# A graph network with 2376 indirect gathers: the gathers lose their bounds check

## The chip, the cores and the metric

The kernel runs on one core of a Trainium2 chip. The metric is device time in microseconds for one execution of the whole program, as the median of several runs.

## The reference

Four graph layers run one after the other on x [100000, 64] with the same 50000 edges (src, dst), sorted by dst. Each layer normalises x, applies relu, gathers rows by src or dst, combines them per edge, sums them per dst and adds the result to x.

```python
edge_index = jnp.stack([src, dst])
h = jnp.maximum(_layernorm(x, axis=-1), 0.0)
x = x + _L0_gnn_ref(h, node_type_4, src, dst, edge_type_8, ...)   # typed attention, softmax per dst
h = jnp.maximum(_layernorm(x, axis=-1), 0.0)
x = x + _L1_gnn_ref(h, proj_cosim, W_ffn, b_ffn, src, dst)        # h[src] - h[dst], gated, two segment sums
h = jnp.maximum(_layernorm(x, axis=-1), 0.0)
x = x + _L2_gnn_ref(h, edge_index, W0, b0, W1, b1)                # (h + segment_sum(h[src])) through an MLP
h = jnp.maximum(_layernorm(x, axis=-1), 0.0)
x = x + _L3_gnn_ref(h, Wq, ..., src, dst)                         # four attention heads
return x
```

## The kernel before

Nodes that no edge points to need no gathers, so their whole path is computed once for all nodes by a dense pass, and the rows of the nodes that do receive edges are then replaced by scatters at the end. The edges are padded to 50688, which is 99 groups of GE = 512, and a group is laid out as TU = 4 blocks of 128 edges, one edge per partition. The nodes are padded to 101376, 99 groups of 1024.

The program is a row of stages with a barrier between them: tables (L304), dense (L478), scores (L693), softmax, attend (L1019), difference (L1222), propagate (L1401), mlp (L1533) and heads (L1695). A stage writes its order out by hand: for every engine a `body` is called for each of the 99 groups plus a tail, and the groups are staggered between the engines by `st.back(lag)`. Everything is unrolled. The engines are kept in step by semaphores, with U = 3 buffers for a group's tiles.

All indirect DMAs are issued from POOL (the GpSimd engine), one for 128 rows, since an offset is given per partition:

- scores, L733: eight gathers a group from the table T0 (rows of 68 floats) into `sc_xg`, four by src and four by dst. POOL waits for `h_done` (DVE, L192), `ptr_c` and the write of the same buffer of three groups ago.
- difference, propagate, mlp, heads: four gathers a group through the helper `gather` (L1212, issue at L1217) from U1, SD, U2 and U3 (rows of 64 floats) into `df_hs`, `pr_gat`, `ml_gat` and `hd_gat`. POOL runs at most three groups ahead of the engine that uses up the rows.
- dense, L522: four scatters a group of two floats a row into T0; heads, L1743: four scatters a group of 64 floats a row into the output. An index far above the table's size marks an edge that writes nothing, and the bounds check drops it.

The indices of the gathers are computed in tables and softmax, and all of them lie inside their tables, padding included. For each indirect DMA with a bounds check the program holds an instruction ahead of it on POOL, a MOVE, that puts the bound into a register; where a group begins with a wait, the wait or the last of several stands on that MOVE.

## Time and profile before

| | us |
|---|---|
| three runs, median | 6802.56 |
| three runs, lowest and highest | 6772.72, 6810.67 |
| profiled execution, its own time | 6742.33 |
| profiled execution, span from the first to the last instruction | 6740.6 |

| Engine | busy us | share of the span |
|---|---|---|
| PE | 5010.8 | 74% |
| DVE | 4934.0 | 73% |
| POOL | 4537.2 | 67% |
| ACT | 2271.6 | 34% |

The profile is of one execution. An instruction's row tells when its engine worked on it; register, wait and branch instructions are not counted as busy. For a DMA that POOL issues, the busy time is POOL's and not that of the transfer. Idle time ahead of an instruction stands with the one that released it; "issue" means that nothing the profile shows was waited for. POOLq is POOL's sequencer. The mean granted clock of TensorE is 0.745 of full speed over the span.

### The profile page before, as it was taken

The page shows a single profiled execution, that of the slowest core. Times are in us where ns is not written, and L with a number is a line of the kernel's source. Part 1 is how long each engine was busy: PE and PEld are TensorE (multiplying, and loading weights), DVE is VectorE, ACT ScalarE, POOL GpSimd, SP SyncE. Part 2 cuts the span into 40 slices and gives each one's busy share as a digit, 9 for nine tenths or more (in the row PEclk, how much of TensorE's full clock was granted, in tenths as well). Part 3 has the DMA queues.
Part 4 walks back from the last instruction along what each step waited for, and adds up shares of the span by engine and source line. Part 5 has one row for each costly group of instructions (what it writes and reads, how often), then busy time and mean ns, then how long its engine had stood idle before and what let it go on. Part 6 is the DMA issues. An engine that isn't in the chain of part 4 may idle for free. (4 is left out here: it accounts for less than half of the span.)

```text
span 6740.6 us, 68483 instructions
## 1 busy us (share of the span) xinstructions
PE 5010.8 (74%) x17065; PEld 2596.9 (39%) x17065; DVE 4934.0 (73%) x7942; ACT 2271.6 (34%) x5856; POOL 4537.2 (67%) x3884
## 2 busy tenths in 40 slices
PE   0777777588888886888887887555577878878876
PEld 0455555344444442333334444122233334444433
DVE  4899999766766766999996665565566667666666
ACT  0555555322222222334333333122122223333333
POOL 1777777567767762666667887666566657777777
PEclk9777777789999997888885555555587767666676
DMA  9222222233333333555543332344455542222221
GB/s 352 85 95 94 95 94 95 80 71 77 77 77 77 79 72 82 145 143 144 142 132 84 82 82 74 95 106 107 96 140 140 141 122 62 65 65 66 63 58 42
DMA packets 788893, 673.28 MB, mean 100 GB/s; under 512 B 514176, under 2 KB 520906, under 8 KB 788376
## 3 DMA queue, kind: packets, MB, share of 16 engines
q1 hardware_dynamic: 486456, 459.62, 23.4%
q0 software_dynamic: 102464, 90.84, 8.1%
q10 hardware_dynamic: 199584, 118.45, 5.7%
q8 instruction: 145, 2.38, 0.1%
q14 instruction: 244, 2.00, 0.1%
HBM read 396.20 MB, written 276.35 MB: 100 GB/s over the span
## 5 line engine op out<-in xcount | busy, mean ns | idle before, releaser
L733 POOL DMA_INDIRECT sc_xg<-t,keep_gather x792 | 872.9, 1102 | 375.5 <-issue 246.0
L1217 POOL DMA_INDIRECT df_hs<-u,keep_idx x396 | 512.8, 1295 | 129.1 <-issue 108.8
L1217 POOL DMA_INDIRECT hd_gat<-u,keep_idx x396 | 481.7, 1216 | 155.4 <-issue 118.0
L1217 POOL DMA_INDIRECT ml_gat<-u,keep_idx x396 | 398.0, 1005 | 274.9 <-issue 125.5
L1743 POOL DMA_INDIRECT out_x<-hd_x,keep_scat_out x396 | 456.3, 1152 | 153.0 <-issue 119.5
L1217 POOL DMA_INDIRECT pr_gat<-sd,keep_idxsd x396 | 411.4, 1039 | 219.0 <-issue 128.9
L522 POOL DMA_INDIRECT t<-keep_ptr_pay,keep_scat_ptr x396 | 441.4, 1115 | 108.2 <-issue 105.2
L1193 PE MATMUL at_ps_m<-at_vx,keep_weights 128*64 128x512 f32 x792 | 446.8, 717 | 26.4 <-POOL at_vx L1090 26.4
L877 PE MATMUL sc_ps_r<-sc_qx,keep_weights 128*64 128x512 f32 x792 | 394.1, 644 | 84.8 <-DVE sc_prod L794 63.0
L687 PE MATMUL den_ps_m<-keep_weights,den_hid 128*128 128x64 f32 x1584 | 237.5, 313 | 199.6 <-ACT den_hid L643 199.6
L1205 PE MATMUL at_ps_y<-keep_weights,at_agg 64*128 64x256 f32 x792 | 239.0, 451 | 171.2 <-DVE at_ysel L1117 170.9
L1883 PE MATMUL hd_ps_h<-keep_weights,hd_xb 128*128 128x128 f32 x792 | 247.8, 413 | 130.9 <-DVE hd_wn L1826 126.0
L1090 POOL TENSOR_TENSOR at_vx<-at_eq,at_v 128x1024 f32<-128x1024 f32 x99 | 255.6, 2582 | 132.0 <-issue 79.5
L153 DVE SCALAR_TENSOR_TENSOR den_den_n_cent<-den_den_n_sum,den_x 128x512 f32<-128x512 f32 x198 | 334.1, 1687 | 3.6
L654 PE MATMUL den_ps_t<-keep_consts,den_h 128*128 128x128 f32 x792 | 185.1, 384 | 195.8 <-DVE den_h L192 195.5
L687 PEld LDWEIGHTS den_ps_m<-keep_weights,den_hid 128*128 128x128 f32 x1584 | 222.2, 224 | 241.4 <-ACT den_hid L643 241.3
L772 DVE SCALAR_TENSOR_TENSOR sc_qx<-sc_et,keep_consts,sc_ps_q 128x512 f32<-128x512 int32 x396 | 276.8, 740 | 48.1 <-DMA t<-tab_row 26.9
L1078 POOL TENSOR_TENSOR at_y<-at_ysel 128x512 f32<-128x512 f32 x99 | 137.4, 1388 | 245.8 <-DVE at_ysel L1117 245.8
L172 ACT ACTIVATE den_den_n_sq<-den_den_n_cent 128x64 f32<-128x64 f32 x792 | 190.6, 242 | 327.0 <-DVE den_den_n_cent L153 326.9
L1883 PEld LDWEIGHTS hd_ps_h<-keep_weights,hd_xb 128*128 128x128 f32 x792 | 195.7, 304 | 250.1 <-DVE hd_wn L1826 203.1
L871 PE MATMUL sc_ps_q<-sc_ht,keep_weights 128*128 128x512 f32 x396 | 223.3, 692 | 92.0 <-issue 68.3
L794 DVE TENSOR_TENSOR sc_prod<-sc_ps_r,sc_kv 64x512 f32<-64x512 f32 x99 | 67.6, 683 | 306.0 <-DMA tab_types<-in_node_type 202.2
(288 smaller groups left out, 13259.5 us busy)
## 6 DMA issues: line engine op xcount, KB each, us to landing
u<-den_h SPq DMA_DIRECT2D x198, 256.0 KB
t<-tab_row ACTq DMA_DIRECT2D x99, 272.0 KB, 11.3
tab_x<-in_x SPq DMA_DIRECT2D x99, 256.0 KB
den_x<-in_x SPq DMA_DIRECT2D x99, 256.0 KB
out_x<-den_x SPq DMA_DIRECT2D x99, 256.0 KB, 2.6
sc_et<-in_etype_row SPq DMA_DIRECT2D x99, 256.0 KB
at_v<-vt SPq DMA_DIRECT2D x198, 128.0 KB
at_et<-in_etype_row SPq DMA_DIRECT2D x99, 256.0 KB
```

Of the source, the lines that this page charges most:

```text
L153: v.scalar_tensor_tensor(out=self.cent[:, :, :], in0=self.over(self.sum), scalar=-1.0 / D, in1=x, op0=ALU.mult, op1=ALU.add).then_inc(self ...
L522: pool.indirect_dma_start(pairs, bass.IndirectOffsetOnAxis(ap=e.scat_ptr[:, c:c + 1], axis=0), e.ptr_pay[:, c, :], None, bounds_check=NP * ...
L687: m = pe.matmul(ps_m[:, j, :], hid[:, a, c * P:(c + 1) * P], e.W["w1"], start=(j == 0), stop=(j == RN - 1), skip_group_check=True)
L733: pool.indirect_dma_start(xg[i][:, u, :], None, e.T0, bass.IndirectOffsetOnAxis(ap=e.gather0[:, b.n, u:u + 1], axis=0), bounds_check=NP - ...
L772: return v.scalar_tensor_tensor(out=qx[:, r, :], in0=et[b.s][:, :], scalar=e.C["rels"][:, r:r + 1], in1=ps_q[:, :], op0=ALU.is_equal, op1= ...
L877: m = pe.matmul(ps_r[:, :], e.W["att"][:, r * D:(r + 1) * D], qx[:, r, :], start=(r == 0), stop=(r == 3))
L1090: pool.tensor_tensor(vx[i][:, 2:4, :], eq[i][:, :, :], vin[i][:, :].unsqueeze(1).broadcast_to([P, 2, GE]), ALU.mult).then_inc(vx_high, 1)
L1193: m = pe.matmul(ps_m[d.s][:, :], e.W["msg"][:, r * D:(r + 1) * D], vx[d.s][:, r, :], start=(r == 0), stop=(r == 3))
L1205: m = pe.matmul(ps_y[:, u, :, :], agg[f.s][:, u * P:(u + 1) * P], e.W["a"][0:D, :].rearrange("p (t f) -> p t f", t=4), start=(u % 2 == 0), ...
L1217: pool.indirect_dma_start(gat[i][:, u, :], None, table, bass.IndirectOffsetOnAxis(ap=idx_all[:, c:c + 1], axis=0), bounds_check=rows - 1, ...
L1743: pool.indirect_dma_start(e.out, bass.IndirectOffsetOnAxis(ap=e.scat_out[:, c:c + 1], axis=0), x4[i][:, u, :], None, bounds_check=NP - 1, ...
L1883: pe.matmul(ps_h[i][:, u, :], xb[i][:, u * P:(u + 1) * P], e.W["wfx"], start=(u == 0), stop=False, skip_group_check=True)
```

## The change

The 2376 gathers are issued without `bounds_check` and `oob_is_err=False`. The helper `gather` loses the argument `rows` that carried the bound. The two groups of scatters (L522 and L1743) are as they were. In the built program the MOVE ahead of each gather is gone, so POOL's MOVEs fall from 3168 to 792, and a wait that stood on a group's first MOVE stands on the gather itself; the gather's out-of-range mode goes from skipping to error. Otherwise every engine holds the same instructions in the same order, and no data, buffer or semaphore value differs.

```diff
@@ scores
                     for u in range(R):
                         pool.indirect_dma_start(xg[i][:, u, :], None, e.T0,
-                                                bass.IndirectOffsetOnAxis(ap=e.gather0[:, b.n, u:u + 1], axis=0),
-                                                bounds_check=NP - 1, oob_is_err=False).then_inc(gathered[i], 16)
+                                                bass.IndirectOffsetOnAxis(ap=e.gather0[:, b.n, u:u + 1], axis=0)).then_inc(gathered[i], 16)
@@
-def gather(pool, table, idx_all, gat, gathered, st, pos, rows):
+def gather(pool, table, idx_all, gat, gathered, st, pos):
 
     i = st.s
     for u in range(TU):
         c = pos * TU + u
         pool.indirect_dma_start(gat[i][:, u, :], None, table,
-                                bass.IndirectOffsetOnAxis(ap=idx_all[:, c:c + 1], axis=0),
-                                bounds_check=rows - 1, oob_is_err=False).then_inc(gathered[i], 16)
+                                bass.IndirectOffsetOnAxis(ap=idx_all[:, c:c + 1], axis=0)).then_inc(gathered[i], 16)
@@ difference (propagate, mlp and heads likewise)
-                    gather(pool, e.U1, e.idx1, hs, gathered, st, pos(st), 2 * EP)
+                    gather(pool, e.U1, e.idx1, hs, gathered, st, pos(st))
```

## Rows read from the trace of the kernel before

**Rows 1.** The page's first part: busy time, share of the span, instructions.

```profile
PE 5010.8 (74%) x17065; PEld 2596.9 (39%) x17065; DVE 4934.0 (73%) x7942; ACT 2271.6 (34%) x5856; POOL 4537.2 (67%) x3884
```

**Rows 2.** Busy time by stretch: scores, difference, heads.

```profile
core 0: us, PE busy (x) PEld busy (x) DVE busy (x) ACT busy (x) POOL busy (x), PEclk, DMA share, GB/s
...
1301.00:2545.00 1244.00, 1042.74 (x3863) 512.95 (x3864) 839.89 (x1367) 336.76 (x582) 872.94 (x792) 0.91 0.37 75
...
3551.00:4195.00 644.00, 526.35 (x1770) 304.60 (x1770) 419.98 (x496) 206.71 (x690) 512.76 (x396) 0.50 0.32 81
...
5522.00:6710.00 1188.00, 935.90 (x2740) 484.15 (x2740) 793.53 (x1268) 446.12 (x882) 922.02 (x776) 0.70 0.23 63
```

**Rows 3.** Groups of heads' POOL DMAs: count | busy, mean ns | idle before, releasers.

```profile
L1217 POOL DMA_INDIRECT hd_gat<-u,keep_idx x396 | 481.7, 1216 | 155.4 <-issue 118.0 <-POOLq L207 34.9 <-DVE hd_x L1821 2.4
L1743 POOL DMA_INDIRECT out_x<-hd_x,keep_scat_out x396 | 456.3, 1152 | 153.0 <-issue 119.5 <-DVE hd_x L1821 33.5
```

**Rows 4.** Waits in scores, propagate, mlp: total us, times, longest.

```profile
POOL sc_xg L733 <- DVE sc_h L192: 110.5, 28, 6.2
DVE sc_sc_n_sum L149 <- DMA sc_xg<-t,keep_gather: 23.7, 3, 15.9
...
POOL pr_gat L1217 <- DVE pr_gm L1481: 71.8, 16, 6.6
DVE pr_gm L1481 <- DMA pr_gat<-sd,keep_idxsd: 24.8, 5, 8.0
...
POOL ml_gat L1217 <- DMA xh<-at_xh: 60.9, 27, 3.7
POOL ml_gat L1217 <- PE ml_ps_t L1674: 60.3, 22, 3.2
PE ml_ps_t L1674 <- DMA ml_gat<-u,keep_idx: 22.1, 3, 16.3
```

**Rows 5.** Waits of PE for gathered rows in difference and heads.

```profile
PE df_ps_t L1387 <- DMA df_hs<-u,keep_idx: 121.7, 58, 13.8
...
PE hd_ps_t L1893 <- DMA hd_gat<-u,keep_idx: 121.1, 46, 15.8
```

**Rows 6.** By source line: count, min/median/max ns, first and last start in us.

```profile
L733 POOLq MOVE  x792: 29/29/29, 1300.7 to 2522.4; - x198
L733 POOL DMA_INDIRECT sc_xg<-t,keep_gather x792: 1004/1011/2065, 1301.5 to 2529.9; - x198
...
L1217 POOLq MOVE  x1584: 29/29/29, 3550.6 to 6681.7; - x198
```

**Rows 7.** Timeline in dense: start, duration, instruction, [idle before, releaser].

```profile
703.46 0.68 DVE L581 TENSOR_TENSOR den_x<-den_ps_m,den_x2b 128x512 f32<-128x512 f32 x1
...
704.22 1.27 POOL L519 TENSOR_TENSOR den_x2b<-den_x,keep_weights 128x512 f32<-128x512 f32 x1 [1.83 <-DVE den_x L581]
...
705.64 1.27 POOL L522 DMA_INDIRECT t<-keep_ptr_pay,keep_scat_ptr  x1 [0.15 <-issue]
...
710.06 0.98 POOL L522 DMA_INDIRECT t<-keep_ptr_pay,keep_scat_ptr  x1 [0.30 <-issue]
711.06 1.29 POOL L529 TENSOR_TENSOR den_x3b<-den_x,keep_bfo_beta 128x512 f32<-128x512 f32 x1
```

**Rows 8.** Timeline of POOL in difference.

```profile
3799.51 2.00 POOL L1217 DMA_INDIRECT df_hs<-u,keep_idx  x1 [0.30 <-issue]
3801.81 1.00 POOL L1217 DMA_INDIRECT df_hs<-u,keep_idx  x1 [0.30 <-ACT df_junk_s L1348]
```

**Rows 9.** Timeline of POOL in tables: a direct DMA behind another one.

```profile
24.17 0.57 POOL L348 DMA_DIRECT2D same_prev<-keep_segc  x1
```

**Rows 10.** Timeline in scores: a gather behind a wait.

```profile
2196.52 0.69 DVE L192 SCALAR_TENSOR_TENSOR sc_h<-sc_sc_n_cent,sc_sc_n_rstd 128x512 f32<-128x512 f32 x1
...
2197.98 1.37 POOL L733 DMA_INDIRECT sc_xg<-t,keep_gather  x1 [5.81 <-DVE sc_h L192]
```

**Rows 11.** By source line, the scatters of dense, as in rows 6.

```profile
L522 POOL DMA_INDIRECT t<-keep_ptr_pay,keep_scat_ptr x396: 978/990/1305, 170.2 to 1258.7; - x198
```

More of the change, by code:

```diff
@@ L1426, in body @@
                     wait(pool, gm_done, st.n - (U - 1), e.pool_passed)
-                    gather(pool, e.SD, e.idxsd, gat, gathered, st, st.n, EP)
+                    gather(pool, e.SD, e.idxsd, gat, gathered, st, st.n)
                 run_groups(pool, body, U, 0)
@@ L1563, in body @@
                     wait(pool, t_ready, st.n - (U - 1), e.pool_passed)
-                    gather(pool, e.U2, e.idx2, gat, gathered, st, st.n, EP + NP)
+                    gather(pool, e.U2, e.idx2, gat, gathered, st, st.n)
                 run_groups(pool, body, U, 0)
@@ L1735, in body @@
                         wait(pool, turned, st.n - (U - 1), e.pool_passed)
-                        gather(pool, e.U3, e.idx2, gat, gathered, st, pos(st), EP + NP)
+                        gather(pool, e.U3, e.idx2, gat, gathered, st, pos(st))
                     b = st.back(5)
```

## The prediction

> **What bounds the kernel now.** I read the page first [rows 1]: no engine is full over the span (PE 74%, DVE 73%, POOL 67%), so a share of the whole says little and the stages have to be taken apart. The table by stretch does that; its rows for scores (1244 us), difference (644) and heads (1188) stand here [rows 2]. Propagate and mlp gather too. Tables, dense, softmax and attend hold no gather, so the change can't touch them; dense has scatters, which keep their check.
>
> There are 2376 gathers (792 in scores, 396 in each of the four others) and 792 scatters. One of either occupies POOL for 1.0 to 1.3 us on average, and before it lie about 0.30 us of idle time put down to "issue", which is time with no wait in it [rows 3]. I ask stage by stage whether that is the path. In scores POOL is busy 872.94 us [rows 2] and 792 x 0.30 = 238 us in such gaps, 1111 of 1244, and it waits another 110.5 us for DVE's sc_h; what would show POOL as the bound, DVE waiting for gathered rows, is 23.7 us in 3 waits [rows 4]. In propagate DVE waits 24.8 us in 5 waits, in mlp PE 22.1 us in 3, and POOL itself waits there for others (71.8 us; 60.9 and 60.3 us) [rows 4]. These three are not bound by the gathers. In difference it is otherwise: POOL is busy 512.76 us and 396 x 0.30 = 119 us in gaps, 632 out of 644 [rows 2], and PE waits 121.7 us in 58 waits for df_hs [rows 5]. In heads gathers and scatters take 481.7 + 456.3 us, with 155.4 + 153.0 us of idle time before them, 1246 us and so more than the 1188 of the stretch, since the last scatters lie behind its end [rows 2, 3]; PE waits 121.1 us in 46 waits for hd_gat [rows 5]. So a gather's price shows in the end in two stages, through 396 + 396 = 792 gathers, and the other 1584 have cover.
>
> **The change, part by part.** It has two parts: what stands in the queue, and what the engine does for each gather. No instruction on any engine changes its place.
>
> Part one: with a bounds check each indirect DMA is preceded by a register MOVE that holds the bound. The rows of the two source lines show it: 792 MOVEs for L733 and 1584 for L1217, 29 ns each [rows 6]. All 2376 disappear: 2376 x 0.029 = 69 us of the sequencer. None of this is on the path as long as the sequencer is ahead of the engine, and it is: the last MOVE of scores starts at 2522.4 and the last gather at 2529.9, 7.5 us later, which is more than five gathers [rows 6]. Value: 0. If the cover were gone the price would be the 69 us, and in the two bound stages 792 x 0.029 = 23 us.
>
> The 0.30 us before each indirect DMA is the tempting number, since 2376 x 0.30 = 713 us. Is it the MOVE's? The rows of dense say it isn't: a TENSOR_TENSOR follows an indirect DMA with next to no gap (710.06 + 0.98 = 711.04, next at 711.06), an indirect DMA follows a TENSOR_TENSOR after 0.15, and an indirect DMA follows another after 0.30 [rows 7]. A sequencer that was the cause would show less gap behind a longer instruction; in difference the gap is 0.30 behind a gather of 2.00 us too, and that at the head of a group, where a wait stands as well [rows 8]. So I read the gap as the engine's own start-up for an indirect DMA, which stays. Against that stands one row: a direct DMA on POOL, which has no bound either, starts with no idle time before it and takes 0.57 us [rows 9]. They have no indices, so I can't separate the two causes; part two keeps this open.
>
> A second effect of part one is real but small. Where POOL has run dry and waits, the wait stands on the MOVE, so the DMA is only handed over once the wait is over. In scores DVE's sc_h ends at 2196.52 + 0.69 = 2197.21 and the gather starts at 2197.98, 0.77 us later [rows 10]; a TENSOR_TENSOR in dense starts 0.08 us after the DVE result it waits for (703.46 + 0.68 = 704.14, then 704.22) [rows 7]. Without the MOVE the wait stands on the DMA itself and it can lie ready. Bounds: 0 and 0.77 - 0.08 = 0.69 us each; I take 0.4, since a start-up of 0.15 to 0.30 stays. Such waits: 28 in scores, 16 in propagate, 27 + 22 in mlp [rows 4], 93 x 0.4 = 37 us of POOL. On the path this can be no more than what the others wait for gathers there beyond the filling of the stage: 23.7 - 15.9, 24.8 - 8.0 and 22.1 - 16.3, that is 30 us [rows 4]. Most of POOL's waits come when it is two groups ahead, where an earlier start is not needed. I take 8 us.
>
> The Trainium skill's Perfetto Trace Analysis, "Sequencer Loop" and the part on SWDGE, says the same of the order of things: an engine instruction is pushed into a queue and waits there, and the sequencer goes on to the next; the rows on the MOVEs agree.
>
> Part two: what the engine does for 128 rows. The trace has no gather without a check. Bounds from the nearest rows: above (cheaper), the direct DMA at 0.57 against 1.00 for a gather, so at most 0.43 us for fetching indices, computing addresses and comparing together [rows 6, 9]. Below (dearer), the scatters of dense that take 1.27 instead of 0.98, 0.29 us more for the same 128 rows [rows 7]; I know no reason that excludes some cost for the form that treats an index out of range as an error. Between them I take 0: the shortest scatter of dense takes 978 ns and the shortest gather of scores 1004, though a row is 8 bytes in one and 272 in the other, and though only the scatter has rows to skip [rows 6, 11]. A figure that hardly moves with the work speaks for a fixed course per row, in which a comparison weighs little or is made anyway.
>
> A rule speaks for the other reading. The Trainium skill's DMA: Bandwidth & Descriptors, "SWDGE vs HWDGE vs iDMA", has the descriptors of such DMAs computed by code that runs on GpSimd's cores, one pair for each row; by it a check that is left out is code that is left out, and the gather becomes cheaper. That is rival A. No row of before can tell.
>
> **The sum.** Profiled execution: span 6740.6, time 6742.33, and the three runs have a median of 6802.56, 60 us above it. MOVEs 0, start-up gaps 0, waits that stand on a MOVE -8, generation 0: 6734 for a profiled execution like this one, and 6802.56 - 8 = 6795 against the median. Within 0.5%, 34 us, is about what a measurement of this kernel can tell from no change.
>
> **Rivals.** A, the check costs the engine time. If it is a third of the 0.43 us, 0.14 us, the two bound stages give 792 x 0.14 = 111 us: 6692. The ceiling is what PE waits for the gathers, 121.7 + 121.1 = 243 us [rows 5], since behind it PE is next (526 of 644 us busy in difference, 936 of 1188 in heads) [rows 2]: 6560 at the best. The same holds if the gap of 0.30 goes with the check (792 x 0.30 = 238). For it: the direct DMA at 0.57 with no gap, and some work per row must be there. Against: how alike the minima are. It passes 0.5% from 43 ns per gather.
>
> B, slower: the form without a bound takes a longer course in the generator, in difference and heads, where POOL has no idle time to take it up. At 0.14 us, half of the 0.29, it costs 792 x 0.14 = 111 us: 6914. From 43 ns per gather it shows; above 0.14 us scores joins, whose cover is POOL's 110.5 us of waiting (792 x 0.14).
>
> C, the change does less than it says: the engine compares with the table's size anyway. Then only part one is left, which is the forecast; it counts there.
>
> D, the waits on the MOVE are worth their full 30 us: 6773, still within 0.5%. It counts with the forecast.
>
> **Chances.** Forecast with C and D: 0.51. A: 0.36. B: 0.13. The likeliest case alone spans 6768 to 6830. The range must reach into A: 6640 takes A up to 792 x 0.205 us, about three parts in four of its chance, and 6835 leaves B out. Left out: 0.13 + 0.07. Faster by over 0.5%: 0.36, within: 0.51, slower: 0.13.
>
> **What would show each step.** No MOVE left for the gathers, and the 0.30 us before each of them still there: step one right. If the gap goes to 0 for gathers and stays for scatters, I misread the dense rows. The shortest gather of scores within 20 ns of 1004: part two right; the scatters at 978 are the control. In scores, propagate and mlp the first gather after a wait should start about 0.3 to 0.5 us after its releaser instead of 0.77. Difference 644 and heads 1188 us unchanged. The prediction is wrong if a gather's own time or gap differs by more than 43 ns, or if a stage that I call covered (scores above all) turns out to follow the gathers.

## The result and the profile after

| | before | after |
|---|---|---|
| median of 4 runs each, us | 6798.93 (6772.72 to 6810.67) | 6845.88 (6837.02 to 6850.26) |
| ratio of the medians | | 1.0073, 95% interval 1.0041 to 1.0104 |
| span of the profiled execution | 6740.6 | 6848.5 |

The change costs 0.7% here. The forecast was 6795 and no change that can be measured; the range up to 6835 misses the time. The first result alone would have misled, too: on other chips the same changed kernel is 3% faster than the one before, as the experiments show. The two profiled executions differ by 108 us and the medians by 47: the profiled execution of before took 6742.33 us, less than any of its four timed ones. So the differences by stage below are larger than those between typical executions.

The page of after, first part, and the table by stretch, with the stretches in the same order as [rows 2], and propagate behind difference (columns as there):

```profile
PE 5020.9 (73%) x17065; PEld 2606.2 (38%) x17065; DVE 4929.5 (72%) x7942; ACT 2269.0 (33%) x5856; POOL 4356.0 (64%) x3884
```

```profile
1300.00:2677.00 1377.00, 1097.01 (x3964) 531.38 (x3964) 851.67 (x1386) 348.45 (x598) 845.83 (x792) 0.90 0.34 69
3651.00:4272.00 621.00, 528.59 (x1784) 306.68 (x1784) 418.46 (x502) 204.58 (x696) 425.43 (x396) 0.50 0.34 84
4272.00:4952.00 680.00, 354.25 (x990) 130.39 (x990) 370.05 (x792) 131.71 (x298) 382.91 (x396) 0.50 0.41 96
...
5632.00:6848.00 1216.00, 932.25 (x2772) 492.58 (x2772) 803.63 (x1290) 448.28 (x892) 920.31 (x792) 0.71 0.22 61
```

POOL has lost 4537.2 - 4356.0 = 181 us of work, and the span is longer. From the start of one stage to the start of the next, before and after: scores 1278 and 1377 (+99), difference 651 and 621 (-30), propagate 640 and 680 (+40), mlp 680 and 680, heads 1219 and 1216. All others agree within 2 us. That adds up to +106 of the 108 us by which the spans differ.

Rows of after by source line (engine, operation, count, min/median/max ns) answer [rows 6 and 11]:

```profile
L733 POOL DMA_INDIRECT sc_xg<-t,keep_gather x792: 950/956/1998, 1300.6 to 2622.7; - x198
...
  DVE sc_h L192: 246.8, 57
  issue: 230.4, 734
```

```profile
L1216 POOL DMA_INDIRECT df_hs<-u,keep_idx x396: 939/945/1923, 3651.3 to 4246.0; - x198
L1216 POOL DMA_INDIRECT pr_gat<-sd,keep_idxsd x396: 939/945/1368, 4272.7 to 4915.2; - x198
```

```profile
L522 POOL DMA_INDIRECT t<-keep_ptr_pay,keep_scat_ptr x396: 972/981/1316, 171.3 to 1258.2; - x198
```

No MOVE stands at L733 or L1216. A gather of scores takes 956 ns instead of 1011, 55 less; the scatter of dense, the control, keeps its 980 within 10. The idle time before a gather is still 0.30 us. So the gathers did become cheaper, by more than the 43 ns that the prediction named as its limit. In the waits that answer [rows 4], one by DVE has grown from 202.2 us in 29 waits to 339.7 in 57. Here is its line of before, and behind it the lines of after (total us, times, longest):

```profile
DVE sc_prod L794 <- DMA tab_types<-in_node_type: 202.2, 29, 12.3
```

```profile
DVE sc_prod L793 <- DMA tab_types<-in_node_type: 339.7, 57, 8.9
POOL sc_xg L733 <- DVE sc_h L192: 246.8, 57, 8.7
...
DVE pr_pr_n_sum L149 <- DMA out_x<-den_x: 219.9, 20, 16.6
...
PE sc_ps_r L876 <- DVE sc_prod L793: 170.7, 40, 6.5
```

The DMAs named as releasers there are much older transfers. The instructions wait for PE: sc_prod for the result sc_ps_r, pr_n_sum for pr_ps_x. The profile falls back on an old DMA since PE had long been done. The timeline of propagate in after shows one such place (start, duration, engine, line, instruction, idle before it):

```profile
4521.88 0.68 PE L1526 MATMUL pr_ps_x<-keep_consts,pr_x 64*128 64x64 f32 x4
...
4521.98 0.94 POOL L1216 DMA_INDIRECT pr_gat<-sd,keep_idxsd  x1 [0.30 <-issue]
...
4523.22 0.95 POOL L1216 DMA_INDIRECT pr_gat<-sd,keep_idxsd  x1 [0.30 <-issue]
4524.48 0.95 POOL L1216 DMA_INDIRECT pr_gat<-sd,keep_idxsd  x1 [0.30 <-issue]
...
4529.21 0.68 ACT L1499 ACTIVATE pr_ffn<-pr_ps_f,keep_weights 64x512 f32<-64x512 f32 x1 [6.52 <-issue]
...
4530.74 0.94 POOL L1216 DMA_INDIRECT pr_gat<-sd,keep_idxsd  x1 [0.30 <-issue]
...
4534.83 0.42 DVE L149 TENSOR_REDUCE pr_pr_n_sum<-pr_ps_x 128x4 f32<-128x256 f32 x1 [11.47 <-DMA out_x<-den_x]
```

PE has finished pr_ps_x at 4522.56. DVE has nothing else to do from 4523.36 on and waits for this result alone; it takes it up at 4534.83, 12.3 us after its end. ACT too gets pr_ps_f late. Meanwhile POOL gathers without a break, one each 1.25 us, until it has run its three groups ahead and must stop at 4531.7. I call this a stall. The kernel before has them as well in propagate:

```profile
4235.08 0.69 PE L1528 MATMUL pr_ps_x<-keep_consts,pr_x 64*128 64x64 f32 x4
...
4248.72 0.42 DVE L149 TENSOR_REDUCE pr_pr_n_sum<-pr_ps_x 128x4 f32<-128x256 f32 x1 [12.83 <-DMA out_x<-den_x]
```

The ends of matmuls are modelled in the profile, so one such place proves little. But the trace also holds the times at which semaphores change, and of the 29 places in propagate of before where DVE stands idle for over 3 us behind a finished pr_ps_x, 28 have the change of its semaphore 0.02 to 0.03 us ahead of DVE's start. It is the signal that is late, and not DVE in answering it.

So the cover that the prediction saw in scores, propagate and mlp is in good part not work of the other engines but stalls of this kind. (In mlp of before ACT's ml_hid starts over 3 us late 21 times.) This is what the experiments had to sort out.

### The profile page after: what moved, and what is told of

Same layout as the page of the kernel before. It is cut to its first block and busy times, and to the rows that moved or that the text cites. A ratio compares the mean times of both kernels' runs of the same rounds, so it can differ in the third digit from the quotient of the medians.

```text
span 6848.5 us, 66107 instructions
## 1 busy us (share of the span) xinstructions
PE 5020.9 (73%) x17065; PEld 2606.2 (38%) x17065; DVE 4929.5 (72%) x7942; ACT 2269.0 (33%) x5856; POOL 4356.0 (64%) x3884
## 5 line engine op out<-in xcount | busy, mean ns | idle before, releaser
L733 POOL DMA_INDIRECT sc_xg<-t,keep_gather x792 | 845.8, 1068 | 496.1 <-DVE sc_h L192 246.8
L876 PE MATMUL sc_ps_r<-sc_qx,keep_weights 128*64 128x512 f32 x792 | 438.2, 705 | 209.7 <-DVE sc_prod L793 170.7
L1216 POOL DMA_INDIRECT ml_gat<-u,keep_idx x396 | 380.2, 960 | 297.5 <-issue 103.7
L1216 POOL DMA_INDIRECT pr_gat<-sd,keep_idxsd x396 | 382.9, 967 | 286.3 <-DVE pr_gm L1479 145.9
L1216 POOL DMA_INDIRECT hd_gat<-u,keep_idx x396 | 459.1, 1159 | 161.9 <-issue 119.4
L1216 POOL DMA_INDIRECT df_hs<-u,keep_idx x396 | 425.4, 1074 | 178.9 <-issue 109.7
L522 POOL DMA_INDIRECT t<-keep_ptr_pay,keep_scat_ptr x396 | 439.7, 1110 | 108.3 <-issue 105.3
L793 DVE TENSOR_TENSOR sc_prod<-sc_ps_r,sc_kv 64x512 f32<-64x512 f32 x99 | 67.6, 683 | 392.8 <-DMA tab_types<-in_node_type 339.7
L876 PEld LDWEIGHTS sc_ps_r<-sc_qx,keep_weights 128*64 128x64 f32 x792 | 118.6, 161 | 523.0 <-issue 522.0
L1521 PE MATMUL pr_ps_f<-pr_agg,keep_weights 64*64 64x512 f32 x198 | 193.7, 1080 | 164.6 <-ACT pr_ffn L1499 128.8
```

What stands on the lines that cost most here:

```text
L522: pool.indirect_dma_start(pairs, bass.IndirectOffsetOnAxis(ap=e.scat_ptr[:, c:c + 1], axis=0), e.ptr_pay[:, c, :], None, bounds_check=NP * ...
L733: pool.indirect_dma_start(xg[i][:, u, :], None, e.T0, bass.IndirectOffsetOnAxis(ap=e.gather0[:, b.n, u:u + 1], axis=0)).then_inc(gathered[ ...
L876: m = pe.matmul(ps_r[:, :], e.W["att"][:, r * D:(r + 1) * D], qx[:, r, :], start=(r == 0), stop=(r == 3))
L1216: pool.indirect_dma_start(gat[i][:, u, :], None, table, bass.IndirectOffsetOnAxis(ap=idx_all[:, c:c + 1], axis=0)).then_inc(gathered[i], 16)
```

## The experiments

Two theories at the start. **Theory H**: the stalls are not the kernel's own doing. They depend on the chip, and so does the sign of the change. **Theory P**: the pace at which gathers follow one another brings the stalls on, and the change quickened it from 1.31 to 1.25 us. They can both be true. The experiments ran in five groups, each on a chip of its own, and the chips turned out to be of two kinds (the first result's is of the first kind, and may be one of the five): the kernel before takes 6717 to 6799 us on the **stalling** kind and 6420 to 6435 on the **smooth** kind. No chip was used for two groups, so a lasting property of the chip and a condition of that hour can't be told apart; "kind of chip" stands for either. Each ratio below is to the kernel before on the same chip.

### The check put back in scores and propagate; the MOVE alone; a shorter run-ahead; a memset between gathers

The first four are edits of the changed kernel; all of them fell on a smooth chip (before: 6423.72).

```diff
# e1: scores, and propagate likewise
-  IndirectOffsetOnAxis(ap=e.gather0[:, b.n, u:u + 1], axis=0)).then_inc(...)
+  IndirectOffsetOnAxis(ap=e.gather0[:, b.n, u:u + 1], axis=0), bounds_check=NP - 1, oob_is_err=False).then_inc(...)
# e2: ahead of every gather
+  pool.reg_mov(bound, NP - 1)
# e3: scores, and propagate likewise
-  wait(pool, h_done, b.n - (U - 1), e.pool_passed)
+  wait(pool, h_done, b.n - 1, e.pool_passed)
# e4: ahead of each gather of scores and propagate
+  pool.memset(spare[:, b.n * R + u, :], 0.0)
```

> The gathers of scores and propagate carry their bounds check again (792 + 396), those of difference, mlp and heads don't. Theory A (each stage's change is its own: gathers that are 55 ns cheaper pay in difference, where POOL is the bound, and hurt in scores and propagate, where POOL only runs further ahead): scores goes back from 1377 to 1278 us and propagate from 680 to 640, difference stays at 622; the total is the changed kernel less 139 us, 6846 - 139 = 6707, about 1.3% below the kernel before's 6799. Rival (the stages differ from execution to execution, or a stage's length depends on what the stages ahead of it did): scores and propagate do not come back, total near 6846.

> No gather carries a bounds check, but ahead of each stands a MOVE to a register of POOL that nothing reads, so the queue looks as it did before, with a group's wait on the MOVE. Theory A (the engine's own time per gather is what changed, and the pace of POOL does the harm): gathers stay at 945 to 956 ns and their gap at 0.30, scores stays at 1377 us and propagate at 680, total near 6846. Rival B (the removed MOVE, or the wait that now stands on the gather itself, does the harm): scores back to 1278 and propagate to 640, total near 6707, with difference at 622.

> The changed kernel, in which POOL may run only two groups ahead instead of three in scores and propagate (it waits for the group before the last but one), so unbroken series of gathers are at most 16 in scores and 8 in propagate. Theory A with its mechanism (a stall of about 12 us comes when POOL gathers in a long unbroken series while the other engines are at work): stalls become shorter or rarer, scores well below 1377, perhaps 1250, propagate below 680. Rival C (the stalls are the chain of the other engines' own and POOL's idle time only follows them): no change, or slower by the lost distance, scores 1377 or more.

> The changed kernel with a small memset on POOL ahead of each gather of scores and propagate, which takes about 0.1 us and breaks the series of indirect DMAs; the pace of the gathers is then between 1.23 and 1.35 us instead of 1.26. Theory A: if the pace decides, the result follows it: at 1.315 us per gather scores comes back to about 1278, at 1.26 or less it stays at 1377 or grows. Rival B (MOVE or wait placement): scores stays at 1377 whatever the pace.

| run | median us | ratio, 95% interval | scores | difference | propagate | mlp |
|---|---|---|---|---|---|---|
| e1 check in scores, propagate | 6296.81 | 0.9796, 0.9775 to 0.9817 | 1168 | 544 | 568 | 535 |
| e2 bare MOVE | 6230.44 | 0.9697, 0.9680 to 0.9714 | 1136 | 545 | 547 | 530 |
| e3 run-ahead of two groups (scores, propagate) | 6219.64 | 0.9686, 0.9668 to 0.9704 | 1122 | 544 | 545 | 532 |
| e4 memset between gathers | 6228.83 | 0.9696, 0.9678 to 0.9714 | 1131 | 544 | 544 | 538 |

The whole level was a surprise: the kernel before was 375 us faster than in the first result, and every edit faster still. e2 says nothing of the MOVE: its trace has the 792 MOVEs of the scatters and no others, so the added moves into a register that nothing reads are not in the program that ran. It is that of the changed kernel, and says by accident that on this chip the change is worth -3.0%. e1 prices the check in the two stages that I had called covered: 6296.81 - 6230.44 = 66 us, or 1188 gathers x 56 ns. On this chip they have no cover. e3 and e4 lie within 0.2% of e2, so neither the run-ahead nor an instruction between gathers matters where there are no stalls.

### Both kernels on one chip, and the error mode

Another chip, again a smooth one (before: 6424.95).

```diff
# e7: the kernel before, at both places where gathers are issued
-  bounds_check=rows - 1, oob_is_err=False).then_inc(gathered[i], 16)
+  bounds_check=rows - 1).then_inc(gathered[i], 16)
```

> The kernel before, unchanged, so that its trace stands beside the others of the same chip; its ratio to itself is 1.000 within 0.3%. Theory P (the pace of the gathers makes the long stalls, on every chip): in scores and propagate the late takings of TensorE's results are as frequent here as in the first profile, and the stage takes about 1278 and 640 us. Theory H (the stalls come from outside the kernel, and differ from chip to chip): on a chip where the kernel takes about 6424 us, scores and propagate take near 1170 and 570 us, as with the check restored there alone, and the stalls of 12 us are absent; on a chip where it takes about 6800, they are there.

> The changed kernel, unchanged. The program in which the bare register moves had been left out by the compiler holds the same instructions, and was 0.970 of the kernel before where that took 6424 us; the first result was 1.0073 where it took 6799. Theory H (the sign goes with the chip's stalls): 0.968 to 0.972 where before takes about 6424, 1.004 to 1.010 where it takes about 6800. Theory N (the two programs differ in something that the instructions don't show): 1.007 on either kind of chip.

> Every gather keeps its bound and with it the register move ahead of it, but an index out of range is an error and not skipped. Theory S (the 55 ns of a gather are the work of skipping): a gather takes 945 to 956 ns as without a bound, and the time is that of the changed kernel within 0.3%. Theory B (the 55 ns are the comparison itself, whatever follows it): a gather takes 993 to 1011 ns as before, and the time is that of the kernel before within 0.3%. If it is faster than before but not as fast as the changed kernel with gathers at 950, the register move has a price of its own.

> The changed kernel, with POOL held to two groups ahead of its users in place of three, in scores, propagate and mlp. Theory P (the unbroken series of gathers brings on the stalls): where the changed kernel is slower than before, this one has fewer of them and is faster than it by over 1% (scores back from 1377 to under 1280 us). Theory H: its ratio stays within 0.5% of the changed kernel's on the same chip, 0.969 where before takes 6424 us.

e5, the kernel before: 6420.09, ratio 0.9995 (0.9984 to 1.0005). e6, the changed kernel: 6233.91, ratio **0.9705 (0.9689 to 0.9721)**. e8, changed and run-ahead of two groups in scores, propagate and mlp: 6234.2, the same ratio. Here are e5 and then e6 by stretch (scores, difference, propagate, mlp, heads; columns as in [rows 2]):

```profile
1301.00:2469.00 1168.00, 1065.38 (x3964) 522.55 (x3964) 861.40 (x1386) 340.28 (x599) 881.50 (x793) 0.94 0.40 81
3439.00:4086.00 647.00, 528.95 (x1784) 306.78 (x1784) 421.81 (x502) 209.97 (x696) 508.63 (x396) 0.50 0.32 81
4086.00:4655.00 569.00, 353.56 (x990) 130.54 (x990) 367.45 (x792) 129.27 (x298) 421.58 (x396) 0.50 0.48 115
4655.00:5212.00 557.00, 447.61 (x1980) 205.19 (x1980) 443.14 (x892) 177.58 (x397) 402.04 (x396) 0.91 0.65 164
5212.00:6421.00 1209.00, 933.91 (x2772) 488.24 (x2772) 803.46 (x1290) 449.62 (x892) 936.41 (x792) 0.71 0.23 62
```

```profile
1300.00:2426.00 1126.00, 1045.53 (x3964) 518.97 (x3964) 852.10 (x1386) 338.64 (x598) 840.24 (x792) 0.95 0.40 84
3397.00:3940.00 543.00, 524.98 (x1784) 306.68 (x1784) 421.81 (x503) 203.77 (x696) 404.14 (x396) 0.50 0.38 96
3940.00:4485.00 545.00, 353.49 (x990) 130.51 (x990) 367.96 (x793) 129.27 (x298) 396.03 (x396) 0.50 0.51 120
4485.00:5020.00 535.00, 442.51 (x1980) 203.63 (x1980) 441.32 (x891) 177.52 (x396) 378.36 (x396) 0.92 0.68 171
5020.00:6222.00 1202.00, 944.71 (x2772) 495.56 (x2772) 803.39 (x1290) 449.27 (x892) 924.32 (x792) 0.69 0.23 62
```

The gain is -41 in scores, -104 in difference, -25 in propagate, -21 in mlp, -8 in heads, together -199 of the 199.9 us between the spans. Without stalls POOL binds the gather stages: in e5's scores 881.5 us busy and 792 x 0.30 = 238 us in gaps make 1120 of 1168, and the one who waits is DVE, for gathered rows, in nearly every group. The row below, of e5's waits, was 23.7 us in 3 waits on the first chip [rows 4]:

```profile
DVE sc_sc_n_sum L149 <- DMA sc_xg<-t,keep_gather: 242.8, 97, 15.9
```

At 55 ns a gather, the figure of the first pair of traces, the change should give 792 x 55 = 44 us in scores and 396 x 55 = 22 in propagate and in mlp; it gives 41, 25 and 21. Difference is the odd one, with 104 us or 263 ns a gather.

e7 tells what of a gather the 55 ns are. With the bound kept and the out-of-range mode switched to error a gather is dearer, not cheaper. Its row for scores, and behind it the one of e5:

```profile
L733 POOL DMA_INDIRECT sc_xg<-t,keep_gather x792: 1017/1021/2080, 1301.7 to 2443.1; - x198
```

```profile
L733 POOL DMA_INDIRECT sc_xg<-t,keep_gather x792: 1003/1007/2064, 1301.7 to 2423.3; - x198
```

e7 takes 6459.96, ratio 1.0057 (1.0040 to 1.0074), +35 us, and 2376 x 14 ns = 33 us. So theory B of that text is nearer: the price goes with having a bound. In scores a gather without one takes 955 ns on this chip (e6), so the bound costs 52 ns when an index out of range is skipped and 66 when it is an error. That the two modes differ by 14 ns theory B had not foreseen, and its time, the kernel before's within 0.3%, was missed.

### On a stalling chip: the same kernel again, and the check stage by stage

The third group fell on a stalling chip (before: 6725.69).

```diff
# e11: difference only
-  gather(pool, e.U1, e.idx1, hs, gathered, st, pos(st))
+  gather(pool, e.U1, e.idx1, hs, gathered, st, pos(st), rows=2 * EP)
# e12: scores as in e1, and
-  gather(pool, e.SD, e.idxsd, gat, gathered, st, st.n)
+  gather(pool, e.SD, e.idxsd, gat, gathered, st, st.n, rows=EP)
-  gather(pool, e.U2, e.idx2, gat, gathered, st, st.n)
+  gather(pool, e.U2, e.idx2, gat, gathered, st, st.n, rows=EP + NP)
```

> The changed kernel again, in a run of its own, beside the kernel before on the same chip. Theory H (the stalls in which TensorE's results are taken up late go with the chip): 0.968 to 0.973 where the kernel before takes about 6424 us and its scores 1168; 1.004 to 1.011 where it takes about 6800 and its scores 1278. Theory N (something else than the chip made the first result): a ratio that doesn't go with the time of the kernel before.

> The changed kernel with POOL held to two groups ahead in scores, propagate and mlp. Where the kernel before takes about 6800 us: theory P (an unbroken series of gathers starves the others; what ends it is POOL running dry) gives over 1% less than the changed kernel, since POOL runs dry a group earlier; if the length of the series makes no difference it is within 0.5% of it. Where the kernel before takes about 6424 us both give the changed kernel's time within 0.3%.

> The changed kernel with the check put back in difference alone. There the stage was 647.1 us with and 543.1 without it, 104 us for 396 gathers, 263 ns each and not 55. Theory C (most of it is DVE's scan and POOL's gathers getting in each other's way, set by how they fall in time): the stage is back at 645 to 655 us and the whole 100 to 108 us above the changed kernel. Theory G (the length of the stage hangs on what the stages ahead left): it stays under 600 us.

> The check put back in the three stages that the prediction called covered. Where the kernel before takes 6424 us they are bound by POOL, and 1584 gathers x 55 ns = 87 us put back give 6321 us, ratio 0.984; if they had cover, the time stays at the changed kernel's 6234, ratio 0.970. Where before takes 6800 us, the stalls decide: theory P gives a time below the changed kernel's, since there scores and propagate were shorter with the check, by 99 and 40 us.

| run | median us | ratio, 95% interval | scores | difference | propagate | mlp |
|---|---|---|---|---|---|---|
| e9 the changed kernel | 6783.08 | 1.0085, 1.0059 to 1.0110 | 1351 | 617 | 672 | 676 |
| e10 run-ahead of two groups (scores, propagate, mlp) | 6766.28 | 1.0064, 1.0041 to 1.0086 | 1320 | 616 | 662 | 676 |
| e11 check in difference | 6825.17 | 1.0161, 1.0124 to 1.0197 | 1324 | 641 | 669 | 678 |
| e12 check in scores, propagate, mlp | 6687.59 | 0.9943, 0.9924 to 0.9963 | 1280 | 617 | 639 | 682 |

e9 repeats the first result. The ratio goes with the kind of chip: 1.0073 and 1.0085 where the kernel before takes 6799 and 6726 us, 0.970 on two smooth ones. That is theory H's part. Theory P's part is e12: putting the check back in the stages where it costs POOL time **shortens** them, by 71 us in scores and 34 in propagate, and makes the only kernel of the group that beats both. In mlp it changes little (+6), as in the first pair of traces. Taking up the check in difference brings the stage to 641 us, near the 645 to 655 that theory C foresaw, but from 617 and not from 543, so it costs 24 us and not 104. The whole of e11 lies 42 us above e9 by the medians. The traces can't account for that: the profiled execution of e11 is 5 us shorter than that of e9 (spans 6794.2 and 6799.0), the shortest of e11's four against the longest of e9's. e10 is between the theories: 0.2% less than e9, with 31 us less in scores; the intervals overlap, and the 1% that theory P promised for it did not come.

### The pace without the check

Is it the pace, or some other thing that goes with the check? Tiny memsets ahead of each gather of scores and propagate slow POOL down without a bound. This fell on another stalling chip (before: 6717.05).

```diff
# e13, e14, e15: N = 1, 2, 4, scores and propagate
+  for k in range(N):
+      pool.memset(spare[:, b.n * R + u, k, :], 0.0)      # 2 floats a partition
# e16: e1 again
```

> The changed kernel with one tiny memset on POOL ahead of each gather of scores and propagate, so that no gather follows another directly; a gather starts some 1.27 us after the one before instead of 1.25. Where the kernel before takes about 6424 us: 6229 (0.970), the changed kernel's time within 0.3%. Where it takes 6725 to 6800: theory P (the rate at which gathers follow one another decides) gives scores about midway between 1278 (1.305 us apart) and 1351 (1.25), near 1310; theory U (what counts is that the series is unbroken by another instruction) gives scores under 1280; theory K (the missing check acts in some other way than by the pace) leaves scores at 1350 to 1377.

> The same with two memsets, which puts gathers some 1.39 us apart, further than the 1.305 of the kernel before. Where before takes 6424 us, scores and propagate are bound by POOL and grow by 1188 x 0.12 = 140 us against one memset: 6370. Where it takes 6725 to 6800: theory P gives scores and propagate at or below those of the kernel before (1278 and 640 us), since POOL's own work at that rate is 792 x 1.39 = 1101 us; theory K leaves scores at 1350 or more.

> The same with four memsets, gathers some 1.63 us apart: POOL's own work in scores is 792 x 1.63 = 1291 us and binds on every chip. Where before takes 6424 us: 6230 + 1188 x 0.36 = 6660. Where it takes 6725 to 6800: if the stalls hang on the rate they are gone here, and scores is 1290 to 1320 us, propagate 650; if they come at any rate they add to it, and scores is over 1400.

> The check put back in scores and propagate alone, which gave 0.9796 where the kernel before takes 6424 us: the same is expected on such a chip. Where before takes 6725 to 6800: theory P gives 0.993 to 0.996, as with mlp's check put back too (0.9943), since mlp took 676 us without the check and 682 with it there; if mlp matters, more than 0.997.

The memsets overlap one another, so the spacing came out smaller than the texts foresaw. In e15 it is 1.33 us in scores by the median of all gathers. POOL's timeline there shows how it comes about, in a place where two gathers stand 1.43 us apart:

```profile
1804.93 0.16 POOL L735 MEMSET sc_spare<- 128x2 f32 x3
1805.24 0.96 POOL L736 DMA_INDIRECT sc_xg<-t,keep_gather  x1
1806.20 0.32 POOL L735 MEMSET sc_spare<- 128x2 f32 x4
1806.67 0.96 POOL L736 DMA_INDIRECT sc_xg<-t,keep_gather  x1
```

| run | from one gather to the next, median us in scores / propagate | median us | ratio, 95% interval | scores | propagate |
|---|---|---|---|---|---|
| e13 one memset | 1.27 / 1.26 | 6774.42 | 1.0094, 1.0061 to 1.0127 | 1320 | 670 |
| e14 two | 1.27 / 1.26 | 6806.14 | 1.0133, 1.0116 to 1.0151 | 1384 | 652 |
| e15 four | 1.33 / 1.31 | 6683.86 | 0.9951, 0.9926 to 0.9975 | 1288 | 613 |
| e16 check in scores, propagate | 1.31 / 1.30 | 6689.03 | 0.9964, 0.9942 to 0.9985 | 1262 | 646 |

e15 is the decisive one: no bound on any gather, about the spacing of the kernel before, and the time of the kernels with a check. Theory K (the missing check acts in another way) falls, and so does theory U (the unbroken series), since in e13 and e14 memsets stand between all gathers and the whole gets no faster than e9's 1.0085. Over all traces of scores on stalling chips, one execution of each kernel, the six kernels that space gathers 1.26 to 1.27 us (after, e9, e10, e11, e13, e14) take 1320 to 1384 us, and the four with 1.31 to 1.33 (before, e12, e15, e16) take 1262 to 1288; no value lies between 1288 and 1320. Propagate parts in the same way, 652 to 680 against 613 to 646. At one and the same spacing the stage still varies by up to 64 us (e13 and e14 in scores), so the size of the step is known only roughly.

The waits of DVE that stand for the stalls follow this less well. In propagate of e15 they have all but vanished, where after had 219.9 us and before, with nearly the spacing of e15, 107.5 in 16 waits (first before, then e15):

```profile
DVE pr_pr_n_sum L149 <- DMA out_x<-den_x: 107.5, 16, 12.8
```

```profile
DVE pr_pr_n_sum L149 <- DMA out_x<-den_x: 2.1, 2, 1.5
```

In scores of e9, of e16 and of e15:

```profile
DVE sc_prod L793 <- DMA tab_types<-in_node_type: 308.9, 53, 8.7
```

```profile
DVE sc_prod L793 <- DMA tab_types<-in_node_type: 196.6, 25, 13.7
```

```profile
DVE sc_prod L796 <- DMA tab_types<-in_node_type: 237.8, 39, 15.2
```

So e9, with the faster pace, has more stalls in scores than e16 (53 for 25), though each is shorter. But e15 has 237.8 us in 39 such waits there, hardly less than the 248.7 in 41 of e13, and its stage is 32 us shorter all the same. In propagate I counted over the whole traces the places where DVE's pr_n_sum or ACT's pr_ffn starts over 3 us after all that it waits for and its engine's last instruction have ended: 49 before, 48 after, 47 in e9, 51 in e12 and e16 each, and none in e15. So there the quicker pace made the stalls longer (319 us in all before, 440 after) and not more frequent. And e15 differs from before, e12 and e16 by more than the median spacing can tell (1.31 and 1.30). The mean spacing of gathers in an unbroken row (those under 1.7 us apart) is 1.37 us in e15 and 1.32 to 1.33 in the three others, so a pace taken as a mean may still be the reason, but the memsets themselves may be too. No run parts these two. e16 against e12 (0.9964 and 0.9943, on two chips, with overlapping intervals) shows that mlp's check matters little.

### A slower pace still, and the best of each stage

```diff
# e17: N = 8 in scores, propagate and mlp; e18: N = 4 in propagate and mlp
+  for k in range(N):
+      pool.memset(spare[:, st.n * TU + u, k, :], 0.0)
# e18: scores as in e1
```

> No check on any gather, eight tiny memsets on POOL ahead of each gather of scores, propagate and mlp. Four of them put gathers 1.33 us apart in scores and 1.31 in propagate, and each one beyond two adds 0.03: some 1.43 us. Theory P (the rate decides): where the kernel before takes 6717 to 6800, scores is no longer than with four (1288 us) as long as POOL's own 792 x 1.45 = 1150 us is less, propagate is under 640, and mlp, 676 at 1.25 us apart, is shorter too. If the gain needs just the spacing of the kernel before and not a slower one, scores is back over 1320. Where before takes 6424: POOL binds all three, and they grow by 1584 x 0.18 = 285 us against the changed kernel's 6234: 6519.

> The best of each stage on the kind of chip where the kernel before takes 6717 to 6800: check kept in scores, four memsets ahead of each gather in propagate and mlp, nothing in difference and heads. There theory P gives 6689 (check in scores and propagate) less 33 us of propagate (613 for 646), so 6656 or 0.991, and less if mlp (672) gains as well. Where before takes 6424: 6234 + 792 x 0.052 + 792 x 0.063 = 6325, 0.985.

These two fell on a smooth chip (before: 6434.54) and so tell nothing of the stalls. e17: 6507.04, 1.0113 (1.0096 to 1.0130), with 6519 expected; e18: 6332.8, 0.9840 (0.9824 to 0.9856), with 6325 expected. On a smooth chip the time can be worked out from POOL's spacing; what a pace slower still does on a stalling chip stays untried.

### Difference, the 104 us

The 55 ns explain 22 us of it. The rest is in rows that show what a gather does there. Of e5 (with the check), DVE and POOL:

```profile
3651.78 0.67 DVE L1296 SCALAR_TENSOR_TENSOR df_lastv<-df_same,df_hd 64x512 f32<-64x512 f32 x1
3652.00 1.33 POOL L1217 DMA_INDIRECT df_hs<-u,keep_idx  x1 [0.30 <-issue]
...
3653.57 1.25 DVE L1306 TENSOR_TENSOR_SCAN df_hb<-df_same,df_hb,df_lastv 64x512 f32<-64x512 f32 x1
3653.63 2.00 POOL L1217 DMA_INDIRECT df_hs<-u,keep_idx  x1 [0.30 <-issue]
```

and of e6 (without it):

```profile
3650.70 1.24 POOL L1216 DMA_INDIRECT df_hs<-u,keep_idx  x1 [0.30 <-issue]
...
3652.24 1.25 DVE L1304 TENSOR_TENSOR_SCAN df_hb<-df_same,df_hb,df_lastv 64x512 f32<-64x512 f32 x1
3652.24 0.94 POOL L1216 DMA_INDIRECT df_hs<-u,keep_idx  x1 [0.30 <-issue]
```

In e5 the scan starts 0.06 us ahead of the gather, and the gather takes 2.00 us instead of 1.00. In e6 both start at 3652.24 and the gather keeps its 0.94. This is no single case. In e5 82 of the stage's 396 gathers start 0.04 to 0.14 us behind this scan, and their median is 2.00 us; in e6 91 start within 0.02 us of it and all take 0.94 to 0.95, while the one that starts 0.07 us behind takes 1.94. POOL's busy time in the stage falls from 508.63 to 404.14 us: 396 x 55 ns = 22 of it is the check, 82 the stretching. The Trainium skill's SBUF — State Buffer, "Who interferes with whom", says that a DVE instruction with two SBUF inputs contends with a GpSimd instruction that reads SBUF, since its second input comes through a shared read interface, and that the order of issue decides who blocks. That a gather is such an instruction, since it reads its indices, is my reading and not the page's; with it the rows agree (stretched by 1.0 us behind the scan, not stretched beside it). With the shorter gathers the two fall into step, and the stage comes down to 543 us, of which PE is busy 525: PE is then the nearest bound. That it is the step between the two and nothing else is what the rows say; no run shifted it alone. e11 had this on the stalling chip: POOL's work in the stage rises with the check and the stage from 617 to 641. That the saving was 104 us on one kind and 24 to 30 on the other goes with stalls: DVE's df_diff starts over 3 us late not once in the two traces of stalling chips with the check in difference (before, e11), and 24 or 25 times in each of the eight without it, 128 to 141 us in all. On smooth chips it never does. No run took these stalls alone away.

## Why the prediction was wrong

- **What bounds the kernel**, the step that failed and that set the sign, was read right for difference and heads, and wrong in what I made of the other three. "These three are not bound by the gathers" held on the chip of the trace. "The other 1584 have cover" doesn't follow: a cover made of late results is not work behind which a saving hides. The sum took these stages at 0 but for the waits; the first pair of traces has +99 us in scores and +40 in propagate, and e12 gives 71 and 34 of that back. I had two signs in hand. One stands in [rows 4]: 60.9 us in which POOL waits for PE in mlp are put down to `xh<-at_xh`, a DMA of attend, which can't be the real releaser. The other is DVE's sc_prod with 202.2 us, put down to a DMA of an early stage. I took POOL's 110.5 us of waiting for slack and did not ask why the waiting ones were late.
- **Part one, the MOVEs**: right. All 2376 are gone, and the gap is 0.30 us with and without them. The waits that stood on a MOVE did get shorter, more than foreseen: in scores of after sc_h ends at 2006.06 + 0.69 = 2006.75 and the gather starts at 2007.02, 0.27 us later for 0.77 before [rows 10]. All 57 gathers of scores that wait for sc_h there start 0.26 us behind its signal, and e16 has both in one execution: 0.76 us in scores, with the check, and 0.26 in mlp, without it. The -8 us for that can't be seen, since the stages with such waits grew.

```profile
2006.06 0.69 DVE L192 SCALAR_TENSOR_TENSOR sc_h<-sc_sc_n_cent,sc_sc_n_rstd 128x512 f32<-128x512 f32 x1
2007.02 1.82 POOL L733 DMA_INDIRECT sc_xg<-t,keep_gather  x1 [4.32 <-DVE sc_h L192]
```

- **Part two, the generation**: "Between them I take 0" is the term of the sum that was mis-sized. It is -55 ns of a possible -430. It is not what missed the time: with it the sum is 6795 - 44 = 6751, further still from 6846. Reading "a comparison weighs little or is made anyway" out of 978 and 1004 ns compared two DMAs that both had the check, so it could say nothing of its price. The Trainium skill's DMA: Bandwidth & Descriptors, "SWDGE vs HWDGE vs iDMA", by which code on GpSimd's cores computes the descriptors, was the better guide; that a check left out is code left out was my step from it, and the 55 ns agree.
- **Rival A** had the mechanism: at 55 ns it gives 792 x 0.055 = 44 us off. Difference and heads together gave 32. Its fault is the same as the forecast's, that nothing outside the two bound stages can move.
- **The sign.** No rival had what happened: gathers that become cheaper and stages that become longer for it. Rival B was slower through dearer gathers, and they aren't. The missing term is +99 us in scores and +40 in propagate, against -30 in difference. e12, e15 and e16 show that it goes away when gathers are issued further apart, with a check or without one. By what means a quicker POOL holds up the signals of PE stays open.
- **The same working on a smooth chip** would have been off the other way: 2376 x 55 ns = 131 us if all stages are bound by POOL, plus 82 us of stretching in difference, less what is hidden (heads gave 8 of 22 us). That comes to 199; measured between the spans of e5 and e6: 199.9. That is no test of it, since the 82 and the 14 are read from these same traces.
- **The range.** Three parts in four of A's 0.36 leave out 0.09 and not 0.07, a slip that changes nothing here.
- **The 0.5% limit** was fair: the ratios of one kernel on chips of one kind agree within 0.2% (0.9697 and 0.9705; 1.0073 and 1.0085). The ratio between kinds does not, and no number of runs on one chip shows that.

## What to carry to other kernels

A bounds check on an indirect DMA costs the engine 52 to 55 ns of 1 us for 128 rows here, so where the indices are known to be in range, leave it out in the stages that the gathers bind. Ahead of a saving on an engine that "has cover", look at what the cover is: if an idle engine's wait is put down to a transfer that ended long ago, results may be taken up late, as here, and quickening their neighbour can make it worse. Here the kernel that is best depends on the chip: check in scores and propagate alone (e1, e16) is 2.0% faster than before on a smooth chip and 0.4% on a stalling one, while no check at all is 3.0% faster on one and 0.7 to 0.9% slower on the other; a figure from one chip doesn't settle such a choice.

## What the runs showed of the hardware

- **Two kinds of chip.** The kernel before took 6717.05, 6725.69 and 6798.93 us in three groups of runs, and 6423.72, 6424.95 and 6434.54 in three others, the five groups of experiments on five chips. Stages without gathers agree: attend 929.5 and 927.5 us, dense 1135.9 and 1135.5. Of the 319 us between the spans 303 lie in scores (1278 and 1168), propagate (640 and 570) and mlp (680 and 557). In mlp the mean granted clock is 0.76 on the stalling chip and 0.91 on the smooth one, and PE is busy 527.6 and 447.6 us, so part of the difference there goes with the clock; whether the stalls lower it or it is a cause of its own no run shows. In propagate it is 0.50 on both.
- **Late results.** On the stalling kind a finished result of PE is taken up by DVE or ACT up to 16.5 us late in stages where POOL issues gathers: 49 places over 3 us in propagate of before, with the engine idle, and 48 in after. In the ten traces of smooth chips there is none. What holds the signal up isn't known. The experiments settle that scores and propagate are longer when POOL's indirect DMAs follow one another in 1.25 to 1.27 us than in 1.31 us and more, and that neither the unbroken series nor the run-ahead decides it.
- **Prices of one indirect DMA of 128 rows of 64 or 68 floats**: 944 to 956 ns with no bound, 997 to 1011 with a bound that skips, 1010 to 1021 with a bound that is an error (medians by stage, heads left out; one chip by itself: 955, 1007 and 1021 in scores); 0.30 us of start-up between two of them, whatever the mode.
- **DVE and POOL**: a gather that starts 0.04 to 0.14 us behind a DVE scan with two SBUF inputs takes 2.00 us instead of 1.00; one that starts within 0.02 us of it is not stretched. POOL lost 82 us of such stretching in one stage when its gathers became 53 ns shorter.
